# Second attention of a four-stage kernel: the RoPE half exchange is issued from ScalarE's DMA queue instead of SyncE's

## The chip, the cores and the metric

One Trainium2 chip, one of its cores. The metric is the device time of one execution in microseconds (us); the value of a kernel is the median of its runs. Before the change it is 2588.01 us over 3 runs (2586.21 to 2594.34).

## The reference

The program is a chain of four residual stages on x of shape (8, 512, 256): attention with LoRA and ALiBi, a top-1 mixture of experts, attention with RoPE, and a feed-forward stage with FP4 quantized operands. Only the third is touched. Its mathematics (T = 512, D = 256, 16 heads of 64):

```python
proj = layernorm(x) @ W_in.T + b_in            # q, k, v: 3 x 1024 columns
q, k = rope(q), rope(k)                        # per head of 64:
#   x_hi, x_lo = x[..., :32], x[..., 32:]
#   y = concat([x_lo * cos + x_hi * sin, x_hi * cos - x_lo * sin])
att = softmax(causal(q @ k.T / 8))
y = (att @ v) @ W_out.T + b_out
x = x + y
```

RoPE needs, beside each vector, the same vector with its two halves of 32 exchanged.

## The kernel before

The stage is `attention1`. It runs over 8 batches, each of 16 heads. A batch has 48 slots: head h has the slots 3h, 3h+1 and 3h+2, and in each slot one group of score tiles (128 rows by 384, 384 or 512 columns) is worked. Every engine has an order written out by hand as a function `slot(b, k, last)`; constants called LAG say how many slots an operation stands behind the one it depends on. All engines run in order, and semaphores connect them.

In one slot k: TensorE computes scores of slot k, transposes the probabilities of slot k-2, multiplies those of slot k-4 with v, and then does side work ("fill") if the slot has some. VectorE takes the row maxima (`row_max`, L959) and the low half of the transposed probabilities (`lo`, L966). ScalarE's slot has, in this order: `value_hi` (L915), `rope_hi` (L909), `hi` (L880), `take` (L894 for q and k, L901 for y, L887 for x), `exp` (L872). TensorE may begin the scores of slot k+2 when `exp` of slot k is done.

q and k are made transposed, features on partitions, and for two heads at a time (a pair: 128 partitions). Pair p needs six slots, 6p to 6p+5. Its q is filled at slot 6p-11 and its k at slot 6p-9; negative numbers are slots of the batch before. One of these is a unit, so a batch has 16 units. The way of a unit is:

- TensorE: 6 matmuls of 512 columns (L809)
- ScalarE, same slot: bias into `t_buf` (L894); VectorE, one slot later: times cosine into `rope` (L988)
- the half exchange: four DMAs, each of 32 partitions x 512 floats, from `t_buf` to `t_sw` ("t_swapped"), L1111
- GpSimd, two slots after the fill: `t_swapped` times sine (L1062), then `rope` plus that (L1065)
- ScalarE, four slots after the fill: `rope_hi` as f16 (L909); GpSimd, five slots after: `rope_lo`, the rest (L1070)
- stacking: DMAs put the parts of q (4, L1120 and L1121) and of k (8, L1123 to L1126) one above the other in `q_stack` and `k_stack`, from which the scores are computed

Both kinds of DMA are issued by the sync engine (SP), in a loop over the pairs of all batches: exchange of q, exchange of k, stacking of q, stacking of k, then the next pair. The stackings wait for `rope_lo`. There are 64 pairs, so 512 exchange DMAs and 768 stacking DMAs.

In batch 0 GpSimd also adds the results of the mixture of experts (L1190, an indirect DMA), one per slot in slots 0 to 3 and 20 to 43.

Of the kernel before, what the change touches and what calls it, by code (L numbers as in the profile page):

```python
# [14 lines left out]
P = 128  # L15
# [62 lines left out]
def wait(eng, sem, value):  # L78

    if isinstance(value, int) and value <= 0:  # L80
        return
    eng.wait_ge(sem, value)
# [534 lines left out]
def attention1(block, x_sb, stats, consts, w, d, sem, sb, banks, aside):  # L617
# [1 line left out]


    LAG_T, LAG_HI, LAG_LO, LAG_PV = 2, 2, 3, 4
    LAG_WA, LAG_WV, LAG_VH, LAG_VL, LAG_W, LAG_ZH, LAG_ZL = 0, 1, 3, 4, 2, 4, 5
    LAG_OUT = LAG_PV + 3
    AT_Q, AT_K, AT_V1, AT_V0, AT_XT, AT_PROJ, YT_LAG = AT1
    DH, HC = DH1, P // DH1
# [21 lines left out]
    t_buf = sb("t_buf", [P, 2, T], F32)  # L647
    t_sw = sb("t_swapped", [P, 2, T], F32)
# [14 lines left out]
    s_t = sem("qk_biased")  # L663
    s_sw = [sem("q_halves_swapped"), sem("k_halves_swapped")]
    s_u = sem("rope_cos_ready")
    s_w = sem("rope_sin_ready")
    s_z = sem("rope_ready")
# [20 lines left out]
    def work(k, last):  # L688

        out = []  # L690
        nxt = [] if last else [1]
        for t, slots in ((0, AT_Q), (1, AT_K)):
            out += [("qk", 0, t, p) for p, at in enumerate(slots) if at == k >= 0]
            for _ in nxt:
                out += [("qk", 1, t, p) for p, at in enumerate(slots) if at < 0 and at + GROUPS == k]
        out += [("V", 0, 1, j) for j, at in enumerate(AT_V1) if at == k]
        for _ in nxt:
            out += [("xT", 1, j) for j, at in enumerate(AT_XT) if at == k]
            out += [("V", 1, 0, j) for j, at in enumerate(AT_V0) if at == k]
        out += [("yT", 0, c) for c in range(CHUNKS) if k == 3 * (HC * (c + 1) - 1) + LAG_OUT + YT_LAG]  # L700
        out += [("proj", 0, i) for i, at in enumerate(AT_PROJ) if at == k]
        return out

    def of(kind, k, last):

        return [(ahead, *a) for kind_, ahead, *a in work(k, last) if kind_ == kind]
# [13 lines left out]
    def bank_of(h, g):  # L720
        return (3 * h + g) % 2

    def unit(b, t, p):
        return (b * PAIRS + p) * 2 + t

    def run(eng, prologue, slot, besides=None):

        prologue()
        for b in range(B):
            last = b == B - 1  # L730
            for k in range(GROUPS):
                if b == 0 and besides:
                    besides(eng, k)
                slot(b, k, last)
                if b > 0 and k + GROUPS < TAIL:
                    slot(b - 1, k + GROUPS, False)
        for k in range(GROUPS, TAIL):
            slot(B - 1, k, True)
# [122 lines left out]
    @block.scalar  # L861
    def _(act):
        work_banks = Banks()

        def exp(b, h, g):
            G = b * GROUPS + 3 * h + g
            wait(act, s_max, G + 1)
            wait(act, s_pt, G - 2)
            off = 0
            for i in GROUP_TILES[g]:  # L870
                L = (i + 1) * P
                last = act.activation(prob[g][:, off:off + L], S[bank_of(h, g)][:, off:off + L], ACT.Exp, bias=neg_max[:, i:i + 1])  # L872
                off += L
            last.then_inc(s_exp, 1)

        def hi(b, h, g):
            G = b * GROUPS + 3 * h + g
            wait(act, s_pt, G + 1)
            wait(act, s_pv, G - 5)
            act.activation(p_hi[g][:, h % 2, :], PT[bank_of(h, g)][:, 0:GROUP_COLS[g]], ACT.Copy).then_inc(s_hi, 1)  # L880

        def take(kind, b, *a):
            bank, n = work_banks.next()
            if kind == "xT":
                j, = a
                wait(act, s_fill, n)
                act.activation(xnT[:, b % 2, :, :, j * P:(j + 1) * P].rearrange("p a c n -> p (a c) n"),  # L887
                               W[bank][:, :].bitcast(F16)[:, 0:2 * D].rearrange("p (k n) -> p k n", n=P),
                               ACT.Copy).then_inc(s_xnT, 1)
            elif kind == "qk":  # L890
                t, p = a
                wait(act, s_fill, n)
                wait(act, s_sw[t], 16 * 4 * (unit(b, t, p) // 2))
                act.activation(t_buf[:, t, :], W[bank][:, :], ACT.Identity, scale=1.0 / W1_SCALE,  # L894
                               bias=w["bias_qk"][:, 0, t * PAIRS + p:t * PAIRS + p + 1]).then_inc(s_t, 1)
            elif kind == "yT":
                c, = a
                wait(act, s_fill, n)
                if b == 0 and c == 0:
                    wait(act, s_wout, 2)  # L900
                act.activation(yT[:, 0, c, :], W[bank][:, :], ACT.Copy).then_inc(s_yTh, 1)  # L901

        def rope_hi(b, t, p):
            U = unit(b, t, p)
            pr = U // 2 - 1
            wait(act, s_z, U + 1)
            if pr >= 0:
                wait(act, (s_qs, s_ks)[t][pr % 2], 16 * (4, 8)[t] * (pr // 2 + 1))
            act.activation(z_hi[:, t, :], rope[:, t, :], ACT.Copy).then_inc(s_zh, 1)  # L909

        def value_hi(b, half, j):
            m = (b * 2 + half) * QT + j
            wait(act, s_vt, m + 1)
            wait(act, s_pv, 3 * (b * HEADS - HEADS + 8 * half + 8))
            act.activation(v_stage[:, half, j, :, 0:64], v_buf[:, j % 2, :].rearrange("p (h d) -> p h d", d=64),  # L915
                           ACT.Copy).then_inc(s_vh, 1)

        def split_out_weights():
            wait(act, s_raw, 16)
            act.activation(w_out[:, 0, :, :], out_raw, ACT.Copy, scale=W1_SCALE).then_inc(s_wout, 1)  # L920

        def prologue():
            for j in range(QT):
                take("xT", 0, j)
            for p in range(2):
                for t in range(2):
                    take("qk", 0, t, p)
                for t in range(2):
                    rope_hi(0, t, p)
            for j in range(QT):  # L930
                take("V", 0, 0, j)
                value_hi(0, 0, j)
            split_out_weights()

        def slot(b, k, last):
            for ahead, half, j in of("V", k - LAG_VH, last):
                value_hi(b + ahead, half, j)
            for ahead, t, p in of("qk", k - LAG_ZH, last):
                rope_hi(b + ahead, t, p)
            if 0 <= k - LAG_HI < GROUPS:  # L940
                hi(b, (k - LAG_HI) // 3, (k - LAG_HI) % 3)
            for kind, ahead, *a in work(k - LAG_WA, last):
                take(kind, b + ahead, *a)
            if k < GROUPS:
                exp(b, k // 3, k % 3)

        run(act, prologue, slot, besides=aside[0])

    @block.vector
# [151 lines left out]
    @block.sync  # L1101
    def _(sp):
        sp.dma_start(out_raw, d["w_out1"].rearrange("(c p) n -> p c n", p=P)).then_inc(s_raw, 16)

        def swap_halves(U):
            t = U % 2
            wait(sp, s_t, U + 1)
            wait(sp, s_z, U - 1)
            for r in range(0, P, 32):
                src = r + 32 if r % 64 == 0 else r - 32  # L1110
                sp.dma_start(t_sw[r:r + 32, t, :], t_buf[src:src + 32, t, :]).then_inc(s_sw[t], 16)  # L1111

        def stack(pr, t):
            U = 2 * pr + t
            wait(sp, s_zl, U + 1)
            wait(sp, s_scores, 6 * (pr - 1))
            for a in range(2):
                hi, lo = z_hi[a * DH:(a + 1) * DH, t, :], z_lo[a * DH:(a + 1) * DH, t, :]
                if t == 0:
                    sp.dma_start(q_st[0:DH, pr % 2, a, :], hi).then_inc(s_qs[pr % 2], 16)  # L1120
                    sp.dma_start(q_st[DH:P, pr % 2, a, :], lo).then_inc(s_qs[pr % 2], 16)  # L1121
                else:
                    sp.dma_start(k_st[0:DH, pr % 2, 0, a, :], hi).then_inc(s_ks[pr % 2], 16)  # L1123
                    sp.dma_start(k_st[DH:P, pr % 2, 0, a, :], lo).then_inc(s_ks[pr % 2], 16)
                    sp.dma_start(k_st[0:DH, pr % 2, 1, a, :], lo).then_inc(s_ks[pr % 2], 16)
                    sp.dma_start(k_st[DH:P, pr % 2, 1, a, :], hi).then_inc(s_ks[pr % 2], 16)  # L1126

        for pr in range(B * PAIRS):
            for t in range(2):
                swap_halves(2 * pr + t)  # L1130
            for t in range(2):
                stack(pr, t)

# [1144 lines left out]
```

## Time and profile before

| | |
|---|---|
| median of 3 runs | 2588.01 us |
| the profiled execution's own time | 2591.73 us |
| its span, first to last instruction | 2589.9 us |
| mean granted TensorE clock | 0.881 of full speed |
| PE / DVE / ACT / POOL busy | 1960.5 / 1665.5 / 1266.5 / 960.0 us |
| second attention, from the first exchange to the last `yT` copy | 950.9 to 2264.2 us |

Busy time counts instructions that compute; the issue of a DMA is not in it, and shows only on SP's queue (SPq). In a timeline row the first number is the start in us from the span's start, the second the duration, and in brackets stands how long the engine sat idle before it and what ended the idle time. Spans on POOL are rough. The profile is of one execution, and terms taken from it are to be compared with its own 2591.73 us.

### The profile page before, as it was taken

The numbers are of one execution on the slowest core, as the hardware profiler recorded it, in microseconds if no ns is written. First come the engines' busy times: TensorE is split into PE (matmuls) and PEld (weight loads), VectorE is DVE, ScalarE is ACT, GpSimd is POOL, SyncE is SP. The second block draws the span as 40 slices with busy tenths as digits, with TensorE's granted clock in tenths as the row PEclk, the third lists the DMA queues.
The fourth block names the chain that finished last, engine by engine and source line by source line (L and its number), as shares of the span: only waits on it lengthen the run. The fifth ranks groups of instructions, "written<-read, shape, count | busy, mean of one in ns | idle before, by whom it ended". The sixth has DMA issues, their size and how long they took to land. (4 is left out here: it accounts for less than half of the span.)

```text
span 2589.9 us, 50884 instructions
## 1 busy us (share of the span) xinstructions
PE 1960.5 (76%) x17478; PEld 1350.0 (52%) x17479; DVE 1665.5 (64%) x3654; ACT 1266.5 (49%) x2545; POOL 960.0 (37%) x1103
## 2 busy tenths in 40 slices
PE   2989989998369946658777776777868767638999
PEld 1666666666346623435555454545545445525665
DVE  3888888887624434645646555565655655568998
ACT  1666666666424425444545544455454545524443
POOL 4444334440310025764444444444443444232222
PEclk8999999998589977878888888888888888859999
DMA  6000000000422223332222222222222222210000
GB/s 215 2 2 2 2 2 2 2 2 27 168 80 82 82 55 74 76 78 63 73 70 63 70 66 70 62 65 69 68 66 66 69 70 63 54 34 8 16 18 23
DMA packets 137686, 141.12 MB, mean 54 GB/s; under 512 B 27696, under 2 KB 114896, under 8 KB 137472
## 3 DMA queue, kind: packets, MB, share of 16 engines
q1 hardware_dynamic: 130816, 128.45, 18.6%
q0 software_dynamic: 6656, 9.85, 1.8%
q8 instruction: 129, 2.11, 0.4%
q14 instruction: 85, 0.70, 0.1%
HBM read 35.71 MB, written 18.61 MB: 21 GB/s over the span
## 5 line engine op out<-in xcount | busy, mean ns | idle before, releaser
L966 DVE TENSOR_TENSOR p_lo_sb<-a_bank,p_hi_sb 128x384 f16<-128x384 f32 (+1 forms) x384 | 228.1, 596 | 346.9 <-ACT p_hi_sb L880 346.2
L756 PE MATMUL a_bank<-k_stack_sb,q_stack_sb 128*128 128x128 f16 (+3 forms) x512 | 162.7, 330 | 329.3 <-ACT prob_sb L872 269.8
L1062 POOL TENSOR_TENSOR t_swapped_sb<-t_swapped_sb,sin_sb 128x512 f32<-128x512 f32 x128 | 164.3, 1284 | 526.2 <-DMA t_swapped_sb<-t_buf_sb 526.2
L872 ACT ACTIVATE prob_sb<-a_bank,neg_max_sb 128x128 f32<-128x128 f32 (+3 forms) x512 | 254.8, 526 | 75.0 <-DVE neg_max_sb L959 73.4
L457 DVE TENSOR_REDUCE neg_max_sb<-a_bank 128x1 f32<-128x128 f32 (+3 forms) x512 | 235.5, 484 | 86.9 <-PE a_bank L237 83.0
L959 DVE TENSOR_REDUCE neg_max_sb<-a_bank 128x1 f32<-128x128 f32 (+3 forms) x512 | 236.2, 483 | 65.9 <-PE a_bank L758 65.6
L380 ACT ACTIVATE probT_sb<-a_bank 128x512 f32<-128x512 f32 (+1 forms) x384 | 198.9, 527 | 136.0 <-PE a_bank L260 131.2
L809 PE MATMUL a_bank<-xnT_sb,w_in_sb 128*128 128x512 f16 x768 | 248.0, 472 | 11.9 <-DVE v_buf_sb L996 11.0
L909 ACT ACTIVATE rope_hi_sb<-rope_sb 128x512 f16<-128x512 f32 x128 | 80.5, 629 | 352.2 <-POOL rope_sb L1065 352.2
L756 PEld LDWEIGHTS a_bank<-k_stack_sb,q_stack_sb 128*128 128x128 f16 x512 | 51.8, 101 | 370.6 <-ACT prob_sb L872 329.4
L767 PE MATMUL a_bank<-ident_f_sb,prob_sb 128*128 128x128 f32 x1280 | 231.9, 301 | 15.2 <-DVE p_lo_sb L966 13.6
L880 ACT ACTIVATE p_hi_sb<-a_bank 128x384 f16<-128x384 f32 (+1 forms) x384 | 201.6, 526 | 81.4 <-PE a_bank L767 81.4
L767 PEld LDWEIGHTS a_bank<-ident_f_sb,prob_sb 128*128 128x128 f32 x1280 | 154.6, 157 | 53.0 <-issue 31.7
L1070 POOL TENSOR_TENSOR rope_lo_sb<-rope_sb,rope_hi_sb 128x512 f16<-128x512 f32 x128 | 152.5, 1197 | 72.0 <-ACT rope_hi_sb L909 72.0
L785 PE MATMUL a_bank<-v_stage_sb,p_hi_sb 128*128 128x65 f16 x1280 | 169.4, 200 | 0.7 <-DVE p_lo_sb L966 0.7
L786 PE MATMUL a_bank<-v_stage_sb,p_hi_sb 128*128 128x65 f16 x1280 | 169.4, 202 | 0.0
L1065 POOL TENSOR_TENSOR rope_sb<-rope_sb,t_swapped_sb 128x512 f32<-128x512 f32 x128 | 161.7, 1263 | 18.4
L988 DVE SCALAR_TENSOR_TENSOR rope_sb<-a_bank,bias_qk_sb,cos_sb 128x512 f32<-128x512 f32 x128 | 95.9, 749 | 112.7 <-ACT t_buf_sb L894 106.6
L787 PE MATMUL a_bank<-v_stage_sb,p_lo_sb 128*128 128x65 f16 x1280 | 167.8, 199 | 0.0
L757 PE MATMUL a_bank<-k_stack_sb,q_stack_sb 128*128 128x128 f16 (+3 forms) x512 | 167.6, 327 | 0.0
L894 ACT ACTIVATE t_buf_sb<-a_bank,bias_qk_sb 128x512 f32<-128x512 f32 x128 | 87.9, 687 | 145.0 <-PE a_bank L809 144.8
L236 PE MATMUL a_bank<-stack_sb 104*128 104x128 bf16 (+3 forms) x512 | 142.0, 303 | 1.8 <-ACT stack_sb L400 1.1
(265 smaller groups left out, 5201.8 us busy)
## 6 DMA issues: line engine op xcount, KB each, us to landing
t_swapped_sb<-t_buf_sb SPq DMA_DIRECT2D x512, 64.0 KB, 2.0
k_stack_sb<-rope_hi_sb SPq DMA_DIRECT2D x256, 64.0 KB, 2.0
k_stack_sb<-rope_lo_sb SPq DMA_DIRECT2D x256, 64.0 KB, 2.0
q_stack_sb<-rope_hi_sb SPq DMA_DIRECT2D x128, 64.0 KB, 2.0
q_stack_sb<-rope_lo_sb SPq DMA_DIRECT2D x128, 64.0 KB, 2.0
sorted_rows<-zeros_sb SPq DMA_DIRECT2D x1, 4992.0 KB, 22.0
x_in_sb<-sorted_rows SPq DMA_DIRECT2D x39, 128.0 KB, 2.1
sorted_results<-y_moe_sb SPq DMA_DIRECT2D x39, 128.0 KB, 1.7
```

The costliest lines, as they stand in the source:

```text
L380: act.activation(probT[:, (h // 4) % 2, h % 4, T_AT[r]:T_AT[r + 1]], ST[(3 * h + r) % 2][:, 0:T_AT[r + 1] - T_AT[r]], ACT.Exp).then_inc(s_ ...
L457: last = dve.tensor_reduce(neg_max[:, h % 2, i:i + 1], S[(3 * h + g) % 2][:, off:off + L], AX.X, ALU.max, negate=True)
L756: pe.matmul(out, q, k_st[:, pr % 2, 0, h % 2, 0:L], start=True, stop=False)
L767: last = pe.transpose(PT[bank_of(h, g)][:, n * P:(n + 1) * P], prob[g][:, n * P:(n + 1) * P], ident_f[:, :])
L785: pe.matmul(o, hi, v[:, 0:65], start=kt == 0, stop=False)
L786: pe.matmul(o, hi, v[:, 65:130], start=False, stop=False)
L787: last = pe.matmul(o, lo, v[:, 0:65], start=False, stop=kt == i)
L809: last = pe.matmul(out, w["in"][:, w_, c, t * 1024 + p * P:t * 1024 + (p + 1) * P], xnT[:, b % 2, x, c, :], start=n == 0, stop=n == len(te ...
L872: last = act.activation(prob[g][:, off:off + L], S[bank_of(h, g)][:, off:off + L], ACT.Exp, bias=neg_max[:, i:i + 1])
L880: act.activation(p_hi[g][:, h % 2, :], PT[bank_of(h, g)][:, 0:GROUP_COLS[g]], ACT.Copy).then_inc(s_hi, 1)
L959: last = dve.tensor_reduce(neg_max[:, i:i + 1], S[bank_of(h, g)][:, off:off + L], AX.X, ALU.max, negate=True)
L966: dve.tensor_tensor(p_lo[g][:, h % 2, :], PT[bank_of(h, g)][:, 0:GROUP_COLS[g]], p_hi[g][:, h % 2, :], ALU.subtract).then_inc(s_lo, 1)
```

## The change

The function `swap_halves` moves from the sync engine's block to ScalarE's block. ScalarE issues the four DMAs of a unit in the slot after the one that wrote `t_buf` (LAG_SW = 1), ahead of everything else in that slot. It waits for the same two semaphores as SP did: `t_buf` written (now by ScalarE itself), and the GpSimd sum of the last unit of the same kind done. SP's loop keeps only the stackings. In the prologue ScalarE issues the exchange right behind each `take`. Data, semaphores' counts and all other orders are unchanged.

```diff
-    LAG_WA, LAG_WV, LAG_VH, LAG_VL, LAG_W, LAG_ZH, LAG_ZL = 0, 1, 3, 4, 2, 4, 5
+    LAG_WA, LAG_WV, LAG_VH, LAG_VL, LAG_SW, LAG_W, LAG_ZH, LAG_ZL = 0, 1, 3, 4, 1, 2, 4, 5
@@ ScalarE
+        def swap_halves(b, t, p):
+            U = unit(b, t, p)
+            wait(act, s_t, U + 1)
+            wait(act, s_z, U - 1)
+            for r in range(0, P, 32):
+                src = r + 32 if r % 64 == 0 else r - 32
+                act.dma_start(t_sw[r:r + 32, t, :], t_buf[src:src + 32, t, :]).then_inc(s_sw[t], 16)
+
@@ ScalarE, prologue
                 for t in range(2):
                     take("qk", 0, t, p)
+                    swap_halves(0, t, p)
@@ ScalarE, slot
+            for ahead, t, p in of("qk", k - LAG_SW, last):
+                swap_halves(b + ahead, t, p)
             for ahead, half, j in of("V", k - LAG_VH, last):
@@ SyncE
-        def swap_halves(U):
-            t = U % 2
-            wait(sp, s_t, U + 1)
-            wait(sp, s_z, U - 1)
-            for r in range(0, P, 32):
-                src = r + 32 if r % 64 == 0 else r - 32
-                sp.dma_start(t_sw[r:r + 32, t, :], t_buf[src:src + 32, t, :]).then_inc(s_sw[t], 16)
-
         for pr in range(B * PAIRS):
-            for t in range(2):
-                swap_halves(2 * pr + t)
             for t in range(2):
                 stack(pr, t)
```

SP's order in the second attention before, from the last stacking of a pair on (t_swapped is the exchange, q_stack and k_stack the stackings):

```order
L1126 DMA k_stack_sb<-rope_hi_sb 64x512
L1111 DMA t_swapped_sb<-t_buf_sb 32x512 [waits rope_ready_a1,qk_biased_a1]
L1111 DMA t_swapped_sb<-t_buf_sb 32x512 x3
L1111 DMA t_swapped_sb<-t_buf_sb 32x512 [waits rope_ready_a1,qk_biased_a1]
L1111 DMA t_swapped_sb<-t_buf_sb 32x512 x3
L1120 DMA q_stack_sb<-rope_hi_sb 64x512 [waits rope_lo_ready_a1]
L1121 DMA q_stack_sb<-rope_lo_sb 64x512
```

and the same place now:

```order
L1129 DMA k_stack_sb<-rope_hi_sb 64x512
L1123 DMA q_stack_sb<-rope_hi_sb 64x512 [waits rope_lo_ready_a1]
L1124 DMA q_stack_sb<-rope_lo_sb 64x512
L1123 DMA q_stack_sb<-rope_hi_sb 64x512
L1124 DMA q_stack_sb<-rope_lo_sb 64x512
L1126 DMA k_stack_sb<-rope_hi_sb 64x512 [waits rope_lo_ready_a1]
```

The eight exchange DMAs of a pair no longer stand between the stackings of one pair and the next.

ScalarE's order from a `rope_hi` of a k unit on, through the slots 1, 2, 3 and 4 of a pair, before:

```order
L909 ACTIVATE rope_hi_sb<-rope_sb 128x512 [waits k_stack_even_ready_a1,rope_ready_a1]
L880 ACTIVATE p_hi_2_sb<-a_bank 128x512 [waits pv_ready_a1,probsT_ready_a1]
L894 ACTIVATE t_buf_sb<-a_bank,bias_qk_sb 128x512 [waits q_halves_swapped_a1,work_filled_a1]
L872 ACTIVATE prob_1_sb<-a_bank,neg_max_sb 128x384 [waits probsT_ready_a1,max_ready_a1]
L915 ACTIVATE v_stage_sb<-v_buf_sb 128x8x64 [waits pv_ready_a1,v_biased_a1]
L880 ACTIVATE p_hi_0_sb<-a_bank 128x384 [waits pv_ready_a1,probsT_ready_a1]
L872 ACTIVATE prob_2_sb<-a_bank,neg_max_sb 128x512 [waits probsT_ready_a1,max_ready_a1]
L880 ACTIVATE p_hi_1_sb<-a_bank 128x384 [waits pv_ready_a1,probsT_ready_a1]
L894 ACTIVATE t_buf_sb<-a_bank,bias_qk_sb 128x512 [waits k_halves_swapped_a1,work_filled_a1]
```

and now:

```order
L917 ACTIVATE rope_hi_sb<-rope_sb 128x512 [waits k_stack_even_ready_a1,rope_ready_a1]
L880 ACTIVATE p_hi_2_sb<-a_bank 128x512 [waits pv_ready_a1,probsT_ready_a1]
L894 ACTIVATE t_buf_sb<-a_bank,bias_qk_sb 128x512 [waits q_halves_swapped_a1,work_filled_a1]
L872 ACTIVATE prob_1_sb<-a_bank,neg_max_sb 128x384 [waits probsT_ready_a1,max_ready_a1]
L909 DMA t_swapped_sb<-t_buf_sb 32x512 [waits rope_ready_a1,qk_biased_a1]
L909 DMA t_swapped_sb<-t_buf_sb 32x512 x3
L923 ACTIVATE v_stage_sb<-v_buf_sb 128x8x64 [waits pv_ready_a1,v_biased_a1]
L880 ACTIVATE p_hi_0_sb<-a_bank 128x384 [waits pv_ready_a1,probsT_ready_a1]
L872 ACTIVATE prob_2_sb<-a_bank,neg_max_sb 128x512 [waits probsT_ready_a1,max_ready_a1]
L880 ACTIVATE p_hi_1_sb<-a_bank 128x384 [waits pv_ready_a1,probsT_ready_a1]
L894 ACTIVATE t_buf_sb<-a_bank,bias_qk_sb 128x512 [waits k_halves_swapped_a1,work_filled_a1]
```

Four DMA issues stand ahead of slot 2's work (and four more ahead of slot 4's); everything else keeps its order. L909 is now the issue, and `rope_hi` has become L917.

## Rows read from the trace of the kernel before

**Rows 1.** The costliest groups of the page (busy, mean ns | idle before, releaser).

```profile
L1062 POOL TENSOR_TENSOR t_swapped_sb<-t_swapped_sb,sin_sb 128x512 f32<-128x512 f32 x128 | 164.3, 1284 | 526.2 <-DMA t_swapped_sb<-t_buf_sb 526.2
L909 ACT ACTIVATE rope_hi_sb<-rope_sb 128x512 f16<-128x512 f32 x128 | 80.5, 629 | 352.2 <-POOL rope_sb L1065 352.2
```

**Rows 2.** Timeline, SP's queue, one pair.

```profile
1306.09 0.50 SPq L1120 DMA_DIRECT2D q_stack_sb<-rope_hi_sb  x1
...
1308.61 0.54 SPq L1123 DMA_DIRECT2D k_stack_sb<-rope_hi_sb  x1
...
1313.02 0.60 SPq L1126 DMA_DIRECT2D k_stack_sb<-rope_hi_sb  x1
1313.72 4.98 SPq L1111 DMA_DIRECT2D t_swapped_sb<-t_buf_sb  x8
1324.08 0.50 SPq L1120 DMA_DIRECT2D q_stack_sb<-rope_hi_sb  x1
```

**Rows 3.** Timeline, GpSimd and ScalarE, the same pair.

```profile
1309.14 0.69 ACT L894 ACTIVATE t_buf_sb<-a_bank,bias_qk_sb 128x512 f32<-128x512 f32 x1 [1.69 <-PE a_bank L809]
...
1317.65 1.26 POOL L1062 TENSOR_TENSOR t_swapped_sb<-t_swapped_sb,sin_sb 128x512 f32<-128x512 f32 x1 [5.62 <-DMA t_swapped_sb<-t_buf_sb]
1320.35 0.63 ACT L909 ACTIVATE rope_hi_sb<-rope_sb 128x512 f16<-128x512 f32 x1 [4.79 <-POOL rope_sb L1065]
1322.90 1.16 POOL L1070 TENSOR_TENSOR rope_lo_sb<-rope_sb,rope_hi_sb 128x512 f16<-128x512 f32 x1
```

**Rows 4.** Lines L1111 (duration in ns min/median/max; landing) and L1573 alone.

```profile
L1111 SPq DMA_DIRECT2D t_swapped_sb<-t_buf_sb x512: 507/590/2002, 950.9 to 2233.4; - x171
DMA to landing us min/median/max: 1.9/2.0/4.0
...
L1573 SPq DMA_DIRECT2D x_in_sb<-sorted_rows x39: 327/339/432, 727.4 to 899.3; - x39
```

**Rows 5.** Busy time by stretch: batch, output projection, pair behind it, pair, two gather pairs.

```profile
core 0: us, PE busy (x) PEld busy (x) DVE busy (x) ACT busy (x) POOL busy (x), PEclk, DMA share, GB/s
1207.24:1364.74 157.50, 117.20 (x1124) 82.10 (x1122) 92.63 (x201) 79.84 (x165) 68.01 (x57) 0.87 0.28 68
1340.60:1359.97 19.37, 17.73 (x161) 13.86 (x162) 11.46 (x27) 9.71 (x21) 8.39 (x7) 0.85 0.28 69
1359.97:1376.48 16.51, 16.09 (x168) 11.48 (x166) 12.82 (x27) 10.55 (x22) 5.93 (x5) 1.00 0.23 56
1381.03:1393.93 12.90, 10.46 (x99) 6.90 (x99) 11.65 (x26) 10.18 (x21) 6.88 (x6) 0.87 0.23 58
1084.60:1136.90 52.30, 31.88 (x258) 20.35 (x258) 25.02 (x57) 19.76 (x41) 36.91 (x27) 0.79 0.42 81
```

**Rows 6.** Timeline, TensorE, two fills of six matmuls after a stall.

```profile
1306.57 2.53 PE L809 MATMUL a_bank<-xnT_sb,w_in_sb 128*128 128x512 f16 x6
1311.51 1.46 PE L809 MATMUL a_bank<-xnT_sb,w_in_sb 128*128 128x512 f16 x6
```

**Rows 7.** Timeline, ScalarE, one place of the order, one batch apart.

```profile
1207.24 0.60 ACT L901 ACTIVATE yT_sb<-a_bank 128x512 f16<-128x512 f32 x1 [1.52 <-PE a_bank L825]
1364.74 0.60 ACT L901 ACTIVATE yT_sb<-a_bank 128x512 f16<-128x512 f32 x1 [1.52 <-PE a_bank L825]
```

**Rows 8.** ScalarE's groups in the batch 1207.24 to 1364.74.

```profile
L894 ACT ACTIVATE t_buf_sb<-a_bank,bias_qk_sb 128x512 f32<-128x512 f32 x16 | 11.0, 688 | 20.4 <-PE a_bank L809 20.4
L909 ACT ACTIVATE rope_hi_sb<-rope_sb 128x512 f16<-128x512 f32 x16 | 10.1, 629 | 39.4 <-POOL rope_sb L1065 39.4
```

**Rows 9.** Timeline, SP's queue and ScalarE, prologue, second pair.

```profile
960.76 1.25 ACT L894 ACTIVATE t_buf_sb<-a_bank,bias_qk_sb 128x512 f32<-128x512 f32 x2
968.99 4.98 SPq L1111 DMA_DIRECT2D t_swapped_sb<-t_buf_sb  x8
975.62 0.63 ACT L909 ACTIVATE rope_hi_sb<-rope_sb 128x512 f16<-128x512 f32 x1 [13.61 <-POOL rope_sb L1065]
```

## The prediction, as recorded before the change was run

> **What bounds the kernel now.** I read the costliest groups of the page first. Two idle times in them belong together: GpSimd sits idle 526.2 us ahead of the sine product, always for the exchange DMA, and ScalarE sits idle 352.2 us ahead of `rope_hi`, always for GpSimd's sum [rows 1]. Nothing else on ScalarE is waited for that long, and ScalarE is in order: while it stands before `rope_hi` it does no `exp`, so TensorE and VectorE stop as well.
>
> Next, why the exchange is late. SP's queue over one pair shows it [rows 2]: q stacking from 1306.09, k stacking from 1308.61 to 1313.62, the eight exchanges from 1313.72 to 1318.70, and then nothing until 1324.08. The q unit's `t_buf`, however, was there at 1309.83 [rows 3]. So its exchange started 3.9 us after it could have, behind the stackings of the pair before, and the k exchange stood behind that. The rest is a closed loop. The fourth q exchange starts at about 1313.72 + 3 x 0.63 = 1315.6, it lands 2.0 us later [rows 4], GpSimd starts at 1317.65, `rope_hi` runs at 1320.35, `rope_lo` at 1322.90 to 1324.06, and at 1324.08 SP begins the next stackings [rows 2, 3]. From 1306.09 to 1324.08 is 18.0 us for one pair, of which SP issues for 20 x 0.63 = 12.6 us. The loop, not the throughput of an engine, sets the pace: between the stalls ScalarE gets through six slots in 12.90 us (the stretch from 1381.03) [rows 5].
>
> Each stall also costs afterwards. The six matmuls of a fill take 2.53 us just behind the stall, and 1.46 us in the next fill [rows 6]; these are TensorE's two clock levels of 1.2 and 2.4 GHz, and the batch's mean granted clock is 0.87 [rows 5].
>
> **The unit of the sum: one batch.** One place of the order comes at 1207.24 and again at 1364.74 [rows 7], 157.5 us. ScalarE is busy 79.84 us of it [rows 5]. Of its 77.7 us idle, 39.4 is the wait at `rope_hi` and 20.4 the wait for TensorE's fill at `t_buf` [rows 8]; some 18 are scattered waits.
>
> **What the change removes.** The exchange no longer stands behind the stackings. A unit's four issues begin one slot after its fill and take 4 x 0.63 = 2.5 us, land 2.0 us on, GpSimd needs 2.7 us (1317.65 to 1320.35): 7.2 us. `rope_hi` stands three slots after the issue begins. Between the last issue and `rope_hi` ScalarE has the rest of one slot and two whole ones, 2.6 slots of 10.18/6 = 1.7 us (busy time of that same stretch) [rows 5], 4.4 us. For q the k issues lie in between as well, 6.9 us against the 4.7 of landing and GpSimd, so no wait. For k it is 4.4 against 4.7 plus semaphores: I take 0.4 us of wait per pair, 3.2 us per batch. That replaces the 39.4 us. SP's own work falls to 12 x 0.63 = 7.6 us per pair and stays out of the way: after `rope_lo` of k there are some five slots until the scores want the stack, and it needs 5.0 + 2.0 us.
>
> **What it adds.** ScalarE issues 64 DMAs per batch. No row shows an issue from ScalarE, so I bound it. The nearest row is the same DMA from SP: 590 ns median [rows 4], 0.63 from start to start in a burst [rows 2]. The low end is the cheapest issue in the trace, 339 ns [rows 4], 0.38 with the same gap of 0.04. The high end is twice the burst pitch, 1.26 us, if it had to take turns with SP's issues. I take 0.63, the same transfer: 64 x 0.63 = 40.3 us per batch. Behind each issuing block stand `value_hi`, `hi` and `exp` of that slot, and TensorE waits for that `exp` two slots on.
>
> Cover: if all of ScalarE's remaining waits stayed, a batch would be 157.5 - 39.4 + 40.3 = 158.4 us, no gain at all. If all vanished it would be 79.8 + 40.3 = 120.1. I take the low end and add what I can name, for this reason: the remaining waits are ScalarE being ahead of TensorE, and 2.5 us of issuing in the slot after each `take` is more than the 20.4/16 = 1.3 us it waits at the next one; TensorE's 117.2 us of busy time is also stretched by the low clock, which should rise with the long gaps gone. What stays: the k wait, 3.2; the six slots with the output projection, where TensorE is busy 17.73 of 19.37 us and ScalarE would be at 9.71 + 5.0, so 4.6 us of waiting stay; the pair behind it, 16.51 against 10.55 + 5.0, 1.0. Sum: 120.1 + 3.2 + 4.6 + 1.0 = 128.9, so about 28.6 us less per batch, or (128.9 - 20 - 17)/6 = 15.3 us for a regular pair. Seven batches after the first: -200.
>
> Batch 0: three pairs without gathers gain 28.6/8 = 3.6 each, -11. In the four with gathers GpSimd is busy 36.91 us in two pairs, 18.5 each, of 26.15 [rows 5]; it becomes the bound, and with some gaps I put them at 20.5: -22. Prologue: `t_buf` of the second pair is done at 962.0, its exchange starts at 968.99 and `rope_hi` runs at 975.62 [rows 9]; 7 us of lateness go, 6 counted. Total -200 - 33 - 6 = -239.
>
> 2591.7 - 239 = 2352.7 for an execution like the profiled one; that lies 3.7 us above the median, so 2349.
>
> **Two rules of the Trainium skill.** SP's row shows an issue of 0.59 us, and no row tells how much of it is a resource shared with ScalarE [rows 4]. The Trainium skill, "Perfetto Trace Analysis", section "DMA Instruction — HWDGE (DVE, Sync)", says that the descriptor generator is shared by two sequencers and locked for exclusive use, and that the lock wait is inside the profiled duration. That speaks against the change; it is rival A, and its price comes from rows.
>
> The gap from issue to landing is 2.0 us [rows 4], while issuing takes 12.6 of 18.0 us of a pair [rows 2]. The Trainium skill, "DMA: Bandwidth & Descriptors", section "Issuing engines are not separate DMA queues", says that using several issuers only saves the sequencer's time to initiate, usually small beside the transfer. Here the trace disagrees with "small"; by the rule the time would stay at 2588, the low-gain part of rival C.
>
> **Rivals.**
> A. The issues take turns. `rope_lo` of k comes in slot 2 of a pair, when ScalarE issues the q exchanges, so SP's 5.0 us of k stacking lie beside them; the k exchanges come when they are nearly over. 32 of 64 issues would cost 1.26 instead of 0.63: +20.2 per batch, 149.1, a gain of 8.4 x 7 = 59, plus 25 in batch 0 (partly hidden by GpSimd's bound) and 6: about 2499. If a part of it hides under the waits that I have left out, 2470. For it: nothing in the trace of how two queues share; against: DMA engines are far from busy (share 0.28 over the batch [rows 5]), so any turn-taking must come from the issuing alone.
> B. ScalarE's issue is cheap, 0.38 us: 64 x 0.25 = 16 us less per batch. Then the pace between the stalls, 12.9 us per pair, set by TensorE's and VectorE's turns, is the bound: 6 x 13.3 + 19.4 + 16.5 = 115.7 per batch, -92 in seven, about 2257.
> C. The wait moves instead of going: the remaining waits stay on ScalarE because TensorE's scores follow each delayed `exp`. The bound above says 158.4 per batch, about 2570 to 2590. Against it: the wait at `t_buf` is TensorE being late, and ScalarE has filled that time itself.
> D. Slower. All 64 issues cost 1.26 us or more, say because the issue also drains ScalarE. Break-even is 79.8 + 64x + 8.8 = 157.5, x = 1.08 us. At 1.26 a batch is 169.2, +11.7 x 7 = 82: about 2670. The slowest issues of L1111 are 2.0 us, but the median is 0.59 [rows 4].
>
> **Chances.** Forecast 0.52, B 0.16, A 0.20, C 0.06, D 0.06. A measurement tells about 0.3% (8 us) from no change. Faster: forecast, A, B and half of C, 0.91; same 0.03; slower 0.06. The range runs from B's 2255 to 2475, which takes in the milder half of A; the forecast's own range is 2300 to 2400.
>
> **What would show it.** Right: ScalarE's idle time before `rope_hi` falls from 352 us to under 50, and only at k units; the exchange rows stand on ScalarE's queue with about 0.6 us each, right behind the `exp` of the slot that wrote `t_buf`; a regular pair takes about 15 us, the mean clock of the stage rises above 0.90; the four gather pairs are near 20 us with GpSimd nearly always busy; SP waits for `rope_lo` between stackings. Wrong: issue rows of 1 us or more beside SP's stackings (A), pairs of 13 us with TensorE full (B), pairs near 20 us with ScalarE waiting at `hi` and `t_buf` for TensorE more than before (C), TensorE waiting for `exp` behind the issues throughout (D).

## The result, and the profile after

| | before | after |
|---|---|---|
| median of 4 runs | 2587.23 us | 2341.11 us |
| lowest and highest | 2586.21, 2594.34 | 2338.09, 2347.13 |
| span of the profiled execution | 2589.9 us | 2345.3 us |
| mean granted TensorE clock | 0.881 | 0.929 |

The ratio is 0.9046, 95% interval 0.9021 to 0.9071. The forecast was 2349 us, 8 us above the measured median. The profiled execution of each kernel is slower than its median, by 4.5 and 6 us.

First the two waits of [rows 1]. The page of the changed kernel has the wait at the sine product (it is L1073 now):

```profile
L1073 POOL TENSOR_TENSOR t_swapped_sb<-t_swapped_sb,sin_sb 128x512 f32<-128x512 f32 x128 | 167.6, 1309 | 240.0 <-DMA t_swapped_sb<-t_buf_sb 240.0
```

and the view of line L917 alone (`rope_hi`) shows what is left of ScalarE's wait, us and times:

```profile
L917 ACT ACTIVATE rope_hi_sb<-rope_sb x128: 612/629/641, 965.1 to 1993.8; 128x512 f16<-128x512 f32 x128
  POOL rope_sb L1076: 22.0, 10
```

352.2 us have become 22.0. GpSimd's wait has only halved, from 526.2, but it costs little now: ScalarE, which stood behind it, waits 22.0 us for it and not 352.2.

SP's queue over one pair, the answer to [rows 2]:

```profile
1258.95 0.46 SPq L1123 DMA_DIRECT2D q_stack_sb<-rope_hi_sb  x1
1259.46 0.60 SPq L1124 DMA_DIRECT2D q_stack_sb<-rope_lo_sb  x1
1260.10 0.80 SPq L1123 DMA_DIRECT2D q_stack_sb<-rope_hi_sb  x1
1260.94 0.62 SPq L1124 DMA_DIRECT2D q_stack_sb<-rope_lo_sb  x1
1261.67 0.54 SPq L1126 DMA_DIRECT2D k_stack_sb<-rope_hi_sb  x1
...
1266.09 0.60 SPq L1129 DMA_DIRECT2D k_stack_sb<-rope_hi_sb  x1
1272.37 0.46 SPq L1123 DMA_DIRECT2D q_stack_sb<-rope_hi_sb  x1
```

The next pair starts 13.4 us after this one, not 18.0, and SP idles 5.7 us in between. Both are among the shortest rounds of their kernel. Over the same six batches of each trace a pair takes 16.0 us on average now and took 19.9 before. ScalarE meanwhile, with its own queue (ACTq) in the same timeline:

```profile
1258.73 0.69 ACT L894 ACTIVATE t_buf_sb<-a_bank,bias_qk_sb 128x512 f32<-128x512 f32 x1 [0.94 <-PE a_bank L809]
1259.32 0.57 ACT L872 ACTIVATE prob_sb<-a_bank,neg_max_sb 128x384 f32<-128x384 f32 x1
1259.45 0.52 ACTq L909 DMA_DIRECT2D t_swapped_sb<-t_buf_sb  x1
1259.78 0.63 ACT L917 ACTIVATE rope_hi_sb<-rope_sb 128x512 f16<-128x512 f32 x1
1259.99 0.61 ACTq L909 DMA_DIRECT2D t_swapped_sb<-t_buf_sb  x1
1260.30 0.60 ACT L880 ACTIVATE p_hi_sb<-a_bank 128x512 f16<-128x512 f32 x1
1260.64 1.26 ACTq L909 DMA_DIRECT2D t_swapped_sb<-t_buf_sb  x2
1261.99 0.49 ACT L880 ACTIVATE p_hi_sb<-a_bank 128x384 f16<-128x384 f32 x1 [1.10 <-issue]
```

Two things are to be seen. The issues of both queues run side by side: ScalarE's third and fourth last 1.26 us together (0.63 each) while SP issues three of its own, one of which takes 0.80. And the first issue starts at 1259.45, while the `exp` of 1259.32 still runs. At this place, where one batch passes into the next, `rope_hi` (1259.78) and `hi` (1260.30) also stand ahead of the issues in ScalarE's order, and neither has begun: the sequencer, the part of ScalarE that reads the instructions, is ahead of the part that computes, here by two whole activations and most of a third. Inside a batch only the `exp` stands there, and the profile counts an issuing block as some 2.1 us of ScalarE's idle time where the four issues take 2.6:

```profile
1250.92 0.39 ACT L872 ACTIVATE prob_sb<-a_bank,neg_max_sb 128x128 f32<-128x128 f32 x1
1251.08 0.52 ACTq L909 DMA_DIRECT2D t_swapped_sb<-t_buf_sb  x1
1251.16 0.50 ACT L872 ACTIVATE prob_sb<-a_bank,neg_max_sb 128x256 f32<-128x256 f32 x1
1251.62 2.04 ACTq L909 DMA_DIRECT2D t_swapped_sb<-t_buf_sb  x3
1253.76 0.60 ACT L880 ACTIVATE p_hi_sb<-a_bank 128x512 f16<-128x512 f32 x1 [2.09 <-PE a_bank L787]
```

The last row is also a trap: its idle time is put down to TensorE, whose semaphore it waits for too, but ScalarE's sequencer was issuing DMAs until 1253.66. All issues of ScalarE's line L909, in ns, min/median/max:

```profile
L909 ACTq DMA_DIRECT2D t_swapped_sb<-t_buf_sb x512: 514/613/1686, 958.4 to 1988.7; - x171
```

One batch, between the same two places of the order as in [rows 7], and the busy time of that stretch, of the pair stretches behind it (six regular pairs, then the six slots with the projection), and of the four pairs with gathers, as in [rows 5]:

```profile
1165.84 0.60 ACT L901 ACTIVATE yT_sb<-a_bank 128x512 f16<-128x512 f32 x1 [1.52 <-PE a_bank L825]
1290.37 0.60 ACT L901 ACTIVATE yT_sb<-a_bank 128x512 f16<-128x512 f32 x1 [1.52 <-PE a_bank L825]
```

```profile
1165.84:1290.37 124.53, 105.79 (x1124) 75.13 (x1122) 92.36 (x201) 77.92 (x165) 68.00 (x57) 1.00 0.35 86
...
1181.32:1269.66 88.34, 71.29 (x771) 49.00 (x767) 68.66 (x149) 58.62 (x126) 50.66 (x43) 1.00 0.37 91
1269.66:1290.37 20.71, 20.55 (x205) 16.55 (x206) 13.66 (x32) 9.22 (x21) 10.92 (x10) 1.00 0.26 65
...
1049.43:1127.70 78.27, 56.13 (x517) 37.79 (x514) 59.66 (x146) 41.58 (x85) 69.60 (x53) 0.85 0.52 105
```

157.50 us have become 124.53. Both are among the shorter ones of their trace: over six batches 159.3 us have become 127.7 on average. TensorE's busy time fell from 117.20 to 105.79 with the same 1124 instructions, and the granted clock of the stretch rose from 0.87 to 1.00: the low level of 1.2 GHz does not come up in it any more. ScalarE has 77.92 us of its own work and 39.4 us of issues. They add up to 117 of 124.5 us, but 9.1 us of the issues lie beside activations, as in the rows above, so together they cover 108.2 us, and ScalarE does neither for 16.4 us.

### The profile page after: what moved, and what is told of

Read it like the earlier page. It is cut to its first block and busy times, and to the rows that moved or that the text cites. A ratio compares the mean times of both kernels' runs of the same rounds, so it can differ in the third digit from the quotient of the medians.

```text
span 2345.3 us, 50884 instructions
## 1 busy us (share of the span) xinstructions
PE 1890.1 (81%) x17478; PEld 1308.7 (56%) x17479; DVE 1676.5 (71%) x3654; ACT 1253.7 (53%) x2545; POOL 961.4 (41%) x1103
## 5 line engine op out<-in xcount | busy, mean ns | idle before, releaser
L1073 POOL TENSOR_TENSOR t_swapped_sb<-t_swapped_sb,sin_sb 128x512 f32<-128x512 f32 x128 | 167.6, 1309 | 240.0 <-DMA t_swapped_sb<-t_buf_sb 240.0
L756 PE MATMUL a_bank<-k_stack_sb,q_stack_sb 128*128 128x128 f16 (+3 forms) x512 | 152.5, 310 | 139.1 <-ACT prob_sb L872 88.1
L767 PE MATMUL a_bank<-ident_f_sb,prob_sb 128*128 128x128 f32 x1280 | 213.9, 283 | 18.8 <-DVE p_lo_sb L977 17.3
L809 PE MATMUL a_bank<-xnT_sb,w_in_sb 128*128 128x512 f16 x768 | 195.5, 393 | 5.3 <-DVE v_buf_sb L1007 2.8
L1076 POOL TENSOR_TENSOR rope_sb<-rope_sb,t_swapped_sb 128x512 f32<-128x512 f32 x128 | 162.3, 1268 | 18.4
L767 PEld LDWEIGHTS a_bank<-ident_f_sb,prob_sb 128*128 128x128 f32 x1280 | 139.8, 145 | 52.3 <-issue 27.8
L786 PE MATMUL a_bank<-v_stage_sb,p_hi_sb 128*128 128x65 f16 x1280 | 162.3, 198 | 0.0
L785 PE MATMUL a_bank<-v_stage_sb,p_hi_sb 128*128 128x65 f16 x1280 | 161.5, 195 | 0.7 <-DVE p_lo_sb L977 0.7
L787 PE MATMUL a_bank<-v_stage_sb,p_lo_sb 128*128 128x65 f16 x1280 | 160.5, 194 | 0.0
L757 PE MATMUL a_bank<-k_stack_sb,q_stack_sb 128*128 128x128 f16 (+3 forms) x512 | 157.6, 308 | 0.0
L568 POOL TENSOR_TENSOR parts_sb<-rest_sb,one_sb 128x256 bf16<-128x256 f32 x64 | 39.2, 612 | 285.7 <-DVE rest_sb L488 285.7
L258 PE MATMUL a_bank<-stack_sb 104*128 104x512 bf16 (+3 forms) x512 | 141.9, 303 | 1.4 <-ACT probT_sb L380 1.2
L2068 POOL TENSOR_TENSOR pair_q_sb<-pair_quot_sb,pair_scale_sb 128x960 f32<-128x960 f32 (+2 forms) x36 | 59.1, 1641 | 196.4 <-DVE pair_quot_sb L2053 196.4
```

What stands on the lines that cost most here:

```text
L756: pe.matmul(out, q, k_st[:, pr % 2, 0, h % 2, 0:L], start=True, stop=False)
L767: last = pe.transpose(PT[bank_of(h, g)][:, n * P:(n + 1) * P], prob[g][:, n * P:(n + 1) * P], ident_f[:, :])
L786: pe.matmul(o, hi, v[:, 65:130], start=False, stop=False)
L809: last = pe.matmul(out, w["in"][:, w_, c, t * 1024 + p * P:t * 1024 + (p + 1) * P], xnT[:, b % 2, x, c, :], start=n == 0, stop=n == len(te ...
L1073: pool.tensor_tensor(t_sw[:, t, :], t_sw[:, t, :], w["sin"][:, t, :], ALU.mult).then_inc(s_w, 1)
L1076: pool.tensor_tensor(rope[:, t, :], rope[:, t, :], t_sw[:, t, :], ALU.add).then_inc(s_z, 1)
```

## The experiments

All are timed against the kernel before on the same chip, 4 runs each. That kernel's median lay between 2583.7 and 2587.4 us each time, so a difference of a few us from the changed kernel's 2341.11 is not read. "Batch" is the time between the two places of [rows 7].

**What makes an issue on ScalarE cost.** Eight issues per unit instead of four, the same bytes:

```diff
-                act.dma_start(t_sw[r:r + 32, t, :], t_buf[src:src + 32, t, :]).then_inc(s_sw[t], 16)
+                for c in range(0, T, T // 2):
+                    act.dma_start(t_sw[r:r + 32, t, c:c + T // 2], t_buf[src:src + 32, t, c:c + T // 2]).then_inc(s_sw[t], 16)
```

> The change with each exchange DMA cut in two along the columns (32 partitions x 256 floats): 8 issues per unit on ScalarE, the same bytes. Theory (ScalarE is the bound and an issue holds it for 0.6 us): 64 more issues per batch, +35 to +40 us per batch, 2340 + 8 x 37 = about 2640 (2580 to 2660). Rival (the issues lie in idle time of ScalarE): under 2420. Rival (the cost is by bytes): no change.

2648.92 us, ratio to before 1.0255 (1.0215 to 1.0296): slower than before the change. 512 more issues cost 308 us, 0.60 us each, and their own duration is the same for half the bytes:

```profile
L910 ACTq DMA_DIRECT2D t_swapped_sb<-t_buf_sb x1024: 513/612/1717, 954.7 to 2289.2; - x171
```

Two issues per unit instead of four, the same bytes. This copies the halves without exchanging them, so the sine term is computed from the wrong half:

```diff
-            for r in range(0, P, 32):
-                src = r + 32 if r % 64 == 0 else r - 32
-                act.dma_start(t_sw[r:r + 32, t, :], t_buf[src:src + 32, t, :]).then_inc(s_sw[t], 16)
+            for r in range(0, P, 64):
+                act.dma_start(t_sw[r:r + 64, t, :], t_buf[r:r + 64, t, :]).then_inc(s_sw[t], 16)
```

> The change with two DMAs of 64 partitions in place of the four of 32 per unit: the same bytes, half the issues on ScalarE. It copies the halves without exchanging them, so RoPE's sine term uses the wrong half. Theory (ScalarE's issuing is what a batch is made of beside its own work): 32 x 0.64 = 20 us less issuing per batch, down to the pace between the stalls of before, 6 x 12.9 + 19.4 + 16.5 = 113.3 us: 2240 to 2270. Rival (the shared version showed that relieving ScalarE is worth little, because the chain to the stackings or TensorE binds right behind it): 2300 to 2340.

2274.64 us, ratio 0.8789 (0.8750 to 0.8827): 66 us under the change, 5 us above the top of what the theory allowed and well below the rival. The stretch of one batch:

```profile
1155.82:1273.70 117.88, 105.25 (x1124) 76.32 (x1122) 93.97 (x201) 79.79 (x165) 67.72 (x56) 0.99 0.36 91
```

That is 6.7 us less in this batch, and over six batches 118.5 us on average against 127.7, 9.2 us less for some 20 us less issuing. So upwards the cost is full, downwards a little under half of it: just below the change other limits begin. The six slots with the projection, where TensorE is full, gained nothing (22.5 us on average, 21.0 in the change); the regular pairs gained 1.4 us each (13.8 for 15.2) for 2.4 us of issuing taken out.

**Is it the order on SP, or the second queue?** The exchange back on SP, in order of due time (the first pairs are written out and left out here):

```diff
-        for pr in range(B * PAIRS):
-            for t in range(2):
-                swap_halves(2 * pr + t)
-            for t in range(2):
-                stack(pr, t)
+        for pr in range(1, B * PAIRS):
+            stack(pr, 0)
+            swap_halves(2 * (pr + 1))
+            stack(pr, 1)
+            swap_halves(2 * (pr + 1) + 1)
```

> Exchange back on SP, but SP's order is written by due time: stacking of q, exchange of the next q, stacking of k, exchange of the next k. ScalarE issues nothing. Theory (the gain came from taking the exchange out from behind the stackings, and SP's 12.6 us of issuing per pair is itself close to the pace): the q exchange is in time, but the k exchange starts only after 5 us of k stacking and is late by some 3 us per pair, so a pair takes 16 to 17.5 us and the whole 2390 to 2470, between before and after. Rival (the order alone was the fault, SP has room): about 2270, faster than the change, because ScalarE is freed of 40 us per batch. Rival (two queues are needed, order is nothing): 2560 or more.

2522.72 us, ratio 0.9764 (0.9735 to 0.9794), a batch of 150.1 us. The order alone brings 61 of the 246 us; the theory's direction, but 50 us beyond its range. The wait at `rope_hi` is one reason, us, times and longest:

```profile
ACT rope_hi_sb L909 <- POOL rope_sb L1065: 282.9, 99, 13.6
```

Many short waits (99) have taken the place of 63 long ones. TensorE's waits for stackings came on top, which I had not priced:

```profile
1593.52 0.60 SPq L1126 DMA_DIRECT2D k_stack_sb<-rope_hi_sb  x1
1595.64 0.26 PE L756 MATMUL a_bank<-k_stack_sb,q_stack_sb 128*128 128x128 f16 x1 [6.00 <-issue]
```

The releaser "issue" means that the profile named none. But the first scores of a pair are the only ones that wait for the stacks, and in all kernels here none starts earlier than 1.48 us after the issue of that pair's last k stacking has ended on SP; this one starts 1.52 us after it, 1594.12 to 1595.64. In this kernel 54 of the 64 first scores start less than 1.75 us after it, with 172 us of idle time of TensorE before them. In the kernel before it is 17 us in 17, in the change 22 us in 17.

**Is it a closed loop?** Two tests on the kernel before. In the first, q and k are filled one slot earlier; in the second, SP stacks the `rope_hi` parts as soon as they exist:

```diff
-AT1 = (tuple(6 * p - 11 for p in range(HEADS // 2)), tuple(6 * p - 9 for p in range(HEADS // 2)),
-       (5, 11, 14, 17), (29, 32, 35, 41),
+AT1 = (tuple(6 * p - 12 for p in range(HEADS // 2)), tuple(6 * p - 10 for p in range(HEADS // 2)),
+       (5, 11, 17, 21), (29, 33, 35, 41),
```

> The kernel before with nothing but the earlier fills. Theory (a closed loop through SP's queue: exchange, landing, GpSimd, rope_hi, rope_lo, stacking, next exchange, 18 us long wherever it stands in the schedule): no gain, 2560 to 2610. Rival (the exchange was merely late against a schedule, and more lead absorbs it): 2450 or less.

```diff
-            wait(sp, s_zl, U + 1)
-            wait(sp, s_scores, 6 * (pr - 1))
-            for a in range(2):
-                ...
+            for part, z, ready in ((0, z_hi, s_zh), (1, z_lo, s_zl)):
+                wait(sp, ready, U + 1)
+                if part == 0:
+                    wait(sp, s_scores, 6 * (pr - 1))
+                for a in range(2):
+                    src = z[a * DH:(a + 1) * DH, t, :]
+                    if t == 0:
+                        sp.dma_start(q_st[part * DH:(part + 1) * DH, pr % 2, a, :], src).then_inc(s_qs[pr % 2], 16)
+                    else:
+                        sp.dma_start(k_st[part * DH:(part + 1) * DH, pr % 2, 0, a, :], src).then_inc(s_ks[pr % 2], 16)
+                        sp.dma_start(k_st[(1 - part) * DH:(2 - part) * DH, pr % 2, 1, a, :], src).then_inc(s_ks[pr % 2], 16)
```

> The kernel before (all exchanges on SP, in front of the stackings) with the early stacking of the rope_hi parts. Theory (a closed loop through SP's queue, whose length is the time of a pair): the two q stackings from rope_hi no longer wait for rope_lo, which takes 1.16 us, so the loop gets 1.0 to 1.3 us shorter and the whole 65 to 85 us: 2500 to 2525. Rival (SP's total of 12.6 us of issuing per pair, or the exchange's place in the schedule, is the bound): 2570 to 2600.

The earlier fills: 2602.0 us, ratio 1.0052 (1.0031 to 1.0072). No gain, as a loop has it. The time alone does not settle it, since these slots cost 58 us in the changed kernel (below) and could hide a gain. SP's waits in this kernel say more: it waits for `t_buf` 3 times, 16.3 us (before, 16 times, 30.2 us), and for `rope_lo` ahead of the q stackings 62 times, 375.5 us (before 361.1). The exchange's input nearly always lay ready, and a round still took 19.9 us on average. The earlier stackings: 2511.78 us, ratio 0.9711 (0.9678 to 0.9744), 74 us less or 1.15 us per pair. Two issues take 1.1 to 1.3 us, and `rope_lo`, beside which they can now lie, 1.16 [rows 3]. SP's queue in that kernel:

```profile
1301.04 1.14 SPq L1122 DMA_DIRECT2D q_stack_sb<-rope_hi_sb  x2
1304.12 1.10 SPq L1122 DMA_DIRECT2D q_stack_sb<-rope_lo_sb  x2
1307.00 0.46 SPq L1124 DMA_DIRECT2D k_stack_sb<-rope_hi_sb  x1
```

Two q stackings now stand ahead of the wait for `rope_lo`. Lead did not shorten the round, taking two issues out of it did. That the gain fits to 0.1 us is in part luck: the k stackings now wait for k's `rope_hi`, as at 1307.00, 32.6 us in 14 places.

**Where in the slot.** The four issues behind `exp` instead of ahead of `hi`:

```diff
-            for ahead, t, p in of("qk", k - LAG_SW, last):
-                swap_halves(b + ahead, t, p)
             ...
             if k < GROUPS:
                 exp(b, k // 3, k % 3)
+            for ahead, t, p in of("qk", k - LAG_SW, last):
+                swap_halves(b + ahead, t, p)
```

> The change with the four issues at the end of the slot, behind hi and exp, instead of ahead of them; the exchange starts about 1 us later. Theory (ScalarE's issue time is the bound, the RoPE chain has little slack for k): TensorE gets one exp earlier and the next one later, no gain; the wait at rope_hi for k comes up by 0 to 1.4 us per pair, 2340 to 2430. Rival (the bound is TensorE waiting for the delayed exp, not ScalarE's total): faster, about 2300.

2400.74 us, ratio 0.9283 (0.9258 to 0.9307), 60 us above the change. `rope_hi` waits 77.2 us in 45 places instead of 22.0 in 10: 55 us more, about the 60. The chain has about 1 us of slack for k, and this spends it.

**Sharing the exchange.** The q exchange on SP between the stackings, the k exchange on ScalarE:

```diff
             for ahead, t, p in of("qk", k - LAG_SW, last):
-                swap_halves(b + ahead, t, p)
+                if t == 1:
+                    swap_halves(b + ahead, t, p)
...
         for pr in range(1, B * PAIRS):
             stack(pr, 0)
+            swap_q(pr + 1)
             stack(pr, 1)
```

> Work shared: the q exchange is issued by SP between the stacking of q and the stacking of k, the k exchange by ScalarE as in the change. SP issues 16 x 0.63 = 10 us per pair, ScalarE 2.5 us. Theory (ScalarE's issues cost their full time, and only the position on SP counts): ScalarE falls to about 100 us per batch, TensorE's 105.8 us of busy time becomes the bound, a batch takes 112 to 118 instead of 124.5 to 128: 2250 to 2285. Rival (the issues are hidden on ScalarE, or any exchange on SP is late): 2340 or more.

2374.71 us, ratio 0.9189 (0.9165 to 0.9214): 34 us slower than the change, where I had expected 55 to 90 faster. The theory missed. The line of TensorE's scores shows why, first row this kernel, us and times:

```profile
  DMA k_stack_sb<-rope_hi_sb: 97.7, 41
```

In the changed kernel the same row is

```profile
  DMA k_stack_sb<-rope_hi_sb: 16.5, 9
```

Counted as above, with the waits for which the profile names no releaser, it is 109 us in 50 first scores against 22 in 17. The q exchange on SP pushed the k stackings back by 2.5 us, and in the changed kernel they are in time by 1.5 us or less in half of the pairs. Three follow-ups. The same shared version with fills one slot earlier:

> The shared version (q exchange on SP, k exchange on ScalarE) with q and k filled one slot earlier (6p-12 and 6p-10), and two fills of v moved out of their way. In the shared version TensorE waited 97.7 us for k stackings, which SP issues behind the q exchange. Theory (ScalarE was really relieved there, and only the k stacking came late, by about a slot): the wait goes, a batch falls from 130.6 to 113 to 120 us, 2240 to 2300 in all, the fastest so far. Rival (some other cost of the shared issue keeps it): 2340 to 2375.

2360.1 us, ratio 0.9112 (0.9088 to 0.9136). The wait for k stackings went as expected (8.4 us in 7), the time did not. Its counterpart without sharing shows that the earlier fills are bad in themselves:

> The change with the same earlier fills, all exchanges on ScalarE. Theory (ScalarE's 78 us of work and 41 us of issuing fill the batch of 124.5 us, the RoPE chain is in time): same within 0.7%, 2325 to 2355. Rival (the chain to the k stacking binds in the change as well): 2300 or less.

2399.55 us, ratio 0.9278 (0.9253 to 0.9302), 58 us slower than the change; this expectation failed. One row of it: ScalarE's wait for TensorE ahead of the `yT` copy (us, times)

```profile
  PE a_bank L825: 62.2, 49
```

against 16.4 in 10 in the change. The fill now stands in the slot behind that of `yT`, and two fills of v are later. How much of the 58 us is this wait and how much the moved v was not separated. With this schedule on both sides, moving the q exchange to SP gained 39 us (2399.6 to 2360.1). And with all on SP:

> All exchanges on SP in the reordered loop, with the earlier fills. Theory (SP's 12.6 us of issuing per pair plus the k exchange behind 5 us of k stacking): one slot of lead moves all deadlines except the one between the exchange and rope_hi, so the wait at rope_hi stays and the wait for stackings shrinks: 2440 to 2510, still slower than the change. Rival (SP's order alone is enough once there is lead): under 2340.

2515.69 us, ratio 0.9714 (0.9693 to 0.9736), 7 us under the version without lead and 6 us above its range's top.

The last two keep the original slots and stack the `rope_hi` parts early, with the edit shown above. On the shared version:

> The shared version (q exchange on SP between the stackings, k exchange on ScalarE) with the same early stacking of the rope_hi parts. There TensorE waited 97.7 us for k stackings and SP's issues stood in one burst of 10 us behind rope_lo. Theory (ScalarE is relieved by 20 us per batch, and the burst gave it back): the burst starts some 1.2 us earlier, half of the stacking wait goes, 2290 to 2330, below the change. Rival (ScalarE's relief is worth nothing): 2340 to 2375.

2342.47 us, ratio 0.9063 (0.9025 to 0.9101): 32 us gained, level with the change and not below it. This expectation failed too, and the time is in the rival's range: TensorE still waits 74.4 us in 40 places for k stackings, a quarter less and not half. On the change:

> The change, with SP issuing the six stackings of a pair that read rope_hi as soon as rope_hi is there, and only the other six after rope_lo; before, all twelve waited for rope_lo. Theory (in the change ScalarE's work and issues fill 119 of 124.5 us per batch, stackings cost TensorE only 16.5 us in all): a small gain, 2315 to 2340. Rival (the chain up to the stackings is the bound): 2300 or less.

2328.79 us, ratio 0.9006 (0.8991 to 0.9021): 12 us under the change, the fastest version that computes the whole reference.

## Why the prediction was right, and where it was off

**The bound before was the loop.** Shown: with more lead the exchange's input lies ready and the round stays, and two issues taken out of it give 1.15 us per pair. Its length was read from one of the shortest rounds, 18.0 us, where the average is 19.9.

**The removed wait.** 39.4 us per batch was to become 3.2. Over the whole run it became 22.0 us: 12.1 in the prologue, 9.0 in the gather pairs of batch 0, and nothing in the batch looked at. Three of the ten waits are at q units, where only k units were forecast. Its near miss is real, though: 1 us later, it is 77.2.

**The price of an issue.** 0.63 us from start to start, taken from SP, was right: 0.613 us of duration and 2.49 us for a block of four, both medians. Not priced was that the first issue lies beside the running `exp`: 0.57 us per unit or 9 us per batch.

**The sum per batch.** 128.9 forecast, 124.53 measured in the first, 127.7 on average over six ((1931.99 - 1165.84)/6, the last such place being at 1931.99). A regular pair takes 88.34/6 = 14.7 us against 15.3. The six slots with the projection take 20.71 against 20 and are TensorE's (20.55 busy), as said. Over the six batches a regular pair takes 15.2 us.

That the sum fits to 1 us is in part luck. On average over the six batches, ScalarE issues for 31.1 us outside its activations, where the sum had 40.3, and is idle for 18.4 us beside both (the gaps between issues included), where the sum had 8.8. The two errors, of 9 and 10 us, cancel. The forecast that ScalarE's idle time not named would vanish was therefore only half right: apart from `rope_hi` it was 38.3 us before, and 18.4 stay.

**The stretches.** Prologue, from the first `xnT` copy to the first `exp`: 46.8 us to 40.7, -6.1 for -6. Batch 0 up to its seventh `yT` copy: 173.0 to 137.5, -35.5 for -33; its four gather pairs take 78.27/4 = 19.6 us for 20.5, GpSimd being busy for 69.60 of the 78.27, as forecast. The rest of the stage gained 210 us in the span for a forecast 200. The mean granted clock from the first exchange to the last `yT` copy rose from 0.85 to 0.96; what that alone is worth was not separated. Before the stage the changed execution was 7.5 us later than the other; the code there is the same, and I put no cause to it.

**Rival A, turn-taking of the two queues,** did not happen to an extent that counts: 596 ns median for a k stacking on SP beside ScalarE's issues (597 before) and 613 for ScalarE's. Of the 1280 exchange and stacking issues, 121 now take over 0.7 us, before 52, and the mean rose from 0.612 to 0.630 us. So the queues do hold each other up, but by 0.02 us per issue. The Trainium skill ("Perfetto Trace Analysis", "DMA Instruction — HWDGE (DVE, Sync)") has a generator that two sequencers share and that one locks for exclusive use. A lock for the whole of an issue would have doubled those that lie side by side, which the rows do not show; a short one agrees with them.

**Rival B** would have needed issues of 0.38 us. Two issues for four, with still less issuing on ScalarE, ran at 2275, so its 2257 was too low. **Rival C** had about half of it: of ScalarE's other idle time, half stayed. **Rival D's** break-even of 1.08 us per issue agrees with the doubled issues, 2 x 0.61 per former issue, at 2649 where 2670 stood for 1.26.

The Trainium skill ("DMA: Bandwidth & Descriptors", "Issuing engines are not separate DMA queues") says that a second issuer saves only sequencer time, usually small beside the DMA. The first half agrees with the runs; the second does not hold here, since SP's issuing was 12.6 of the 18.0 us of a pair [rows 2], and the change is worth 246 us.

What remains open: why relieving ScalarE of 20 us per batch gives back only 9. The six slots with the projection account for part of it. TensorE's waits for stackings, counted as above, are a small part: 39 us in 23 first scores over the whole run, 17 us more than in the change. No run took the turns between TensorE, VectorE and ScalarE apart.

## What to carry to other kernels

When an in-order queue holds both the last step of one round and the first step of the next, look for the loop that this closes: its length, not any engine's busy time, is then the pace, and a step taken out of the round helps where an earlier start does not. Before moving DMA issues to a compute engine, multiply their count by the issue time of the same transfer in the trace, and lay that beside the engine's busy time of one round, not beside its idle time, part of which is waiting that will be absorbed. And do not expect the whole issue time back when issues go: another limit may lie just below. Then ask which transfer is due next on either queue: here the k chain had 1 to 1.5 us to spare, and the two rearrangements that spent it, the issues behind `exp` and the q exchange on SP, lost 60 and 34 us.

## What the runs showed of the hardware

An issue on ScalarE took 0.61 us for 32 rows of 2048 bytes and for 32 rows of 1024 bytes (613 and 612 ns median). On SP the first took 0.59 (590 ns). For 64 rows of 2048 bytes on ScalarE it was 566 ns, a pair of which shows in the timeline of the kernel with two issues:

```profile
1230.90 1.21 ACTq L908 DMA_DIRECT2D t_swapped_sb<-t_buf_sb  x2
```

So for these copies within the on-chip buffer the count of DMAs is the issuing engine's price, not their size. ScalarE's sequencer issues a DMA while activations before it still run or have not begun: 0.57 us per block of issues lay beside them. Scores that wait for a stacking start 1.5 us after its issue has ended.
